# One decoder layer: v kept token by token in DRAM, a bf16 difference in place of a cast, the second close stage's inputs issued by ScalarE, roots ahead of weight remainders

## The reference

```
x = layernorm(x + L0_attn(x))          # qkv = x @ W + b; phi(q), phi(k) = exp(q @ omega - |q|^2 / 2) / sqrt(128)
                                       # y = phi(q) . cumsum(phi(k) v) / (phi(q) . cumsum(phi(k)) + 1e-6); y @ W_proj + b
x = layernorm(x + L0_xattn(x, ctx))    # causal softmax attention, keys and values preceded by 154 rows of ctx; @ W_proj + b
x = layernorm(x + L0_ffn(x))           # 16 routed experts (top 4, in the best 2 of 4 groups) and 2 shared ones
```

## Time and profile before

| | |
|---|---|
| median of 3 runs | 2140.28 us (2139.8 to 2140.62) |
| the profiled execution | 2145.23 us, of which the span from first to last instruction is 2143.2 us |
| granted TensorE clock, mean | 0.940 |
| busy: PE, DVE, ACT, POOL | 87%, 69%, 43%, 21% of the span |
| second close stage with its surroundings (1370 to 1500 us) | 130 us, PE 63% busy |
| first close stage with its surroundings (530 to 690 us) | 160 us, PE 77%, DVE 79% busy |

### The profile page before, as it was taken

The page is one execution under the profiler, slowest core; times in us unless marked ns, Lnnn a source line. Parts: engine busy times, 40 slices in busy tenths (PEclk is TensorE's granted clock), DMA queues, the critical chain, the costliest instruction groups (busy, mean ns, idle before and its releaser), DMA issues. The chain is left out here.

```text
span 2143.2 us, 39212 instructions
## 1 busy us (share of the span) xinstructions
PE 1874.6 (87%) x13696; PEld 1223.8 (57%) x13696; DVE 1484.2 (69%) x3864; ACT 912.8 (43%) x1398; POOL 439.8 (21%) x629
## 2 busy tenths in 40 slices
PE   7948999997885669989989999765799999999997
PEld 4636676775553123333333333243688788888886
DVE  7934455554786758878878888242788877777776
ACT  5524555553332036656656666711323223323322
POOL 2124233211332321112112111254500000000000
PEclk9979999999998579999999999988899999999999
DMA  6989666661687544534534531465400000000000
GB/s 171 220 143 154 108 108 107 111 161 45 174 234 162 87 54 70 80 51 73 79 51 74 78 59 36 121 200 154 135 1 30 30 5 27 30 30 1 20 11 10
DMA packets 161259, 187.38 MB, mean 87 GB/s; under 512 B 74498, under 2 KB 131538, under 8 KB 154942
## 3 DMA queue, kind: packets, MB, share of 16 engines
q1 hardware_dynamic: 135071, 137.56, 28.1%
q0 software_dynamic: 9952, 31.21, 9.7%
q10 hardware_dynamic: 16063, 16.23, 3.4%
HBM read 114.33 MB, written 70.20 MB: 86 GB/s over the span
## 5 line engine op out<-in xcount | busy, mean ns | idle before, releaser
L1406 ACT ACTIVATE sa_prob<-sa_ps_s 128x1024 f32<-128x1024 f32 (+3 forms) x480 | 376.3, 825 | 314.0 <-PE sa_ps_s L1313 193.8
L1466 DVE CUSTOM_DVE_ANT_0 sa_ps_m<-sa_ps_m,sa_later 128x282 f32<-128x282 f32 (+4 forms) x640 | 278.4, 460 | 87.7 <-PE sa_ps_m L1286 86.4
L1469 DVE TENSOR_REDUCE sa_piece_max<-sa_ps_m 128x1 f32<-128x512 f32 x384 | 259.2, 688 | 35.8 <-PE sa_ps_m L1286 35.2
L1286 PE MATMUL sa_ps_m<-sa_k,sa_q 96*128 96x358 bf16 (+7 forms) x1024 | 259.8, 304 | 8.4 <-DVE sa_piece_max L1466 6.7
L1807 DVE SCALAR_TENSOR_TENSOR mo_acc<-mo_ps_o,mo_keep,mo_acc 128x256 f32<-128x256 f32 x512 | 212.2, 476 | 71.8 <-PE mo_ps_o L215 71.6
L1673 ACT ACTIVATE mo_h_hi<-mo_h 128x512 fp32r<-128x512 f32 x144 | 91.0, 632 | 273.0 <-DVE mo_h L1789 270.8
L1444 POOL TENSOR_SCALAR_AFFINE_SELECT sa_prob<-sa_prob 128x256 f32<-128x256 f32 x256 | 102.5, 406 | 509.7 <-ACT sa_prob L1406 507.1
L1313 PE MATMUL sa_ps_s<-sa_q,sa_k 99*128 99x512 bf16 (+3 forms) x768 | 179.7, 330 | 2.1 <-ACT sa_prob L1406 2.0
L1284 PEld LDWEIGHTS sa_ps_m<-sa_km,sa_q 96*128 96x128 bf16 x512 | 50.8, 100 | 218.7 <-issue 124.9
L683 DVE TENSOR_TENSOR la_att<-la_ps_att,la_cap 128x512 f32<-128x512 f32 x128 | 88.3, 690 | 124.8 <-PE la_ps_att L588 124.8
L1286 PEld LDWEIGHTS sa_ps_m<-sa_k,sa_q 96*128 96x128 bf16 x1024 | 99.0, 100 | 127.6 <-DVE sa_piece_max L1466 48.8
(11 more groups left out here) (197 smaller groups left out, 3893.6 us busy)
## 6 DMA issues: line engine op xcount, KB each, us to landing
sa_q<-s_q_parts SPq DMA_DIRECT2D x96, 128.0 KB, 5.0
la_q<-s_q_parts POOLq DMA_DIRECT2D x90, 128.0 KB, 6.1
la_k<-s_k_parts POOLq DMA_DIRECT2D x90, 128.0 KB, 8.2
sa_k<-s_k_parts SPq DMA_DIRECT2D x84, 128.0 KB, 7.5
s_y<-la_y SPq DMA_DIRECT2D x16, 512.0 KB, 3.5
s_x<-cl_xn SPq DMA_DIRECT2D x16, 512.0 KB, 5.8
s_y<-sa_y SPq DMA_DIRECT2D x16, 512.0 KB, 3.2
mw_raw<-experts SPq DMA_DIRECT2D x18, 384.0 KB, 3.9
```

Source lines behind the costliest of these rows:

```text
L1286: last = nc.tensor.matmul(ps_m[:, s, a - lo:hi - lo], qs, k[g][0:STACK, j, a - MEM:hi - MEM], start=lo > 0, stop=True, skip_group_check=True)
L1406: nc.scalar.activation(dst, src, ACT.Exp, scale=HD ** -0.5).then_inc(expd[s], 1)
L1466: nc.vector.tensor_tensor_reduce(ps_m[:, s, 0:hi - lo], ps_m[:, s, 0:hi - lo], later[:, BANK + lo - first:BANK + hi - first], 1.0, -BIG, A ...
L1469: nc.vector.tensor_reduce(piece_max[:, j, t, n:n + 1], ps_m[:, s, 0:hi - lo], AX.X, ALU.max).then_inc(piece_done[s], 1)
```

## The change

Five edits. (1) v is laid out in DRAM token by token, all 16 heads of a token in one row of 272 floats: one DMA per tile stores it with 1088-byte rows, and the attention stages pick 68 of the 272 floats of each row. (2) In stage 1, for the pair (0, 1) only, the second part is computed as a bf16 difference of `full` and the first part, and not as a cast of the float32 remainder; with it one of the two links of the chain of waits is gone, and the order becomes remainder 0, second part 0, remainder 1, second part 1. (3) In stage 2 the inputs of tile n+2 are issued by ACT at the head of its tile n, no longer by SP. (4) In stage 2 POOL takes the root of tile 2b+1 ahead of the weight remainder. (5) The counts that waits on v's stores compare with follow (1).

```diff
@@ project, store of v (close stage 1 has the same)
-                    for t in range(TB):
-                        rows = v_out.rearrange("(i t) w -> i t w", t=T)[bass.ds(b * QUADS, QUADS),
-                                                                        half * TILE + t * P:half * TILE + (t + 1) * P]
-                        sp.dma_start(rows.rearrange("g t w -> t g w"),
-                                     v[:, half, t].rearrange("p (g h) d -> p g (h d)", g=QUADS)).then_inc(v_out_sem[half], 16)
+                    rows = v_out[bass.ds(b * T + half * TILE, TILE)].rearrange("(n p) w -> p n w", p=P)
+                    sp.dma_start(rows, v[:, half].rearrange("p n h d -> p n (h d)")).then_inc(v_out_sem[half], 16)
@@ linear_attention, load_v (softmax_attention has the same)
-            eng.dma_start(v[pr][:, :, :], io["v"][bass.ds(kk * (SLOTS * T) + pr * T, T)]
+            eng.dma_start(v[pr][:, :, :], io["v"][bass.ds(kk * T, T), pr * VW:(pr + 1) * VW]
@@ close_attention, SP
-                    if not on and more:
-                        load_inputs(sp, b, half)
                     sp.wait_ge(normed[half], b + 1 + START)
@@ close_attention, POOL
                 inputs(b + 1, 0)
+                root(*((b + 1, 0) if on else (b, 1)))
                 if not on:
                     weights.remainder(pool, 2 * b)
-                root(*((b + 1, 0) if on else (b, 1)))
                 inputs(b + 1, 1)
@@ close_attention, ACT
-                    if on and more:
+                    if more:
                         load_inputs(act, b, half)
                     act.wait_ge(t_ps, n + 1 + START)
@@ close_attention, DVE, split
                     ins = nc.vector.tensor_tensor(rest[:, s], full[:, s], parts[:, s, 0], ALU.subtract)
+                    if pair[0] == 0:
+                        ins = nc.vector.tensor_tensor(parts[:, s, 1], full[:, s], parts[:, s, 0], ALU.subtract)
                 chain.link(ins)
-                for s in pair:
-                    ins = nc.vector.tensor_copy(parts[:, s, 1], rest[:, s])
-                chain.link(ins)
+                if pair[0]:
+                    for s in pair:
+                        ins = nc.vector.tensor_copy(parts[:, s, 1], rest[:, s])
+                    chain.link(ins)
@@ scratch
-    "v": ((NQ * T, VW), F32),
+    "v": ((B * T, QUADS * VW), F32),
```

More of the change, by code:

```diff
@@ L308, in _ @@
             for half in range(HALVES):
-                sp.wait_ge(v_out_sem[half], 16 * TB * B + START)
+                sp.wait_ge(v_out_sem[half], 16 * B + START)
                 sp.wait_ge(n_out[half], 16 * B + START)
@@ L435, in _ @@
                     dve.wait_ge(v_ps[half], b + 1 + START)
-                    dve.wait_ge(v_out_sem[half], b * (16 * TB) + START)
+                    dve.wait_ge(v_out_sem[half], b * 16 + START)
                     for t in range(TB):
@@ L811, in batch_row @@
                     sp.wait_ge(v_full, tile(b, half) + 1 + START)
[L812 to L817, removed]
+                    rows = io["v"][bass.ds(b * T + half * TILE, TILE)].rearrange("(n p) w -> p n w", p=P)
+                    sp.dma_start(rows, v[:, half].rearrange("p n h d -> p n (h d)")).then_inc(v_out[half], 16)
             for b in range(B):
@@ L824, in _ @@
                 if on:
-                    sp.wait_ge(v_out[half], 16 * TB * B + START)
+                    sp.wait_ge(v_out[half], 16 * B + START)
                 else:
@@ L1051, in copy_v @@
                 dve.wait_ge(v_ps, tile(b, half) + 1 + START)
-                dve.wait_ge(v_out[half], b * (16 * TB) + START)
+                dve.wait_ge(v_out[half], b * 16 + START)
                 for t in range(TB):
@@ L1213, in load_rest @@
             load_stack(eng, km[g], io["mem_parts"], quad_before(b, g), RIGHT, arrived[g])
-            eng.dma_start(v[g][:, :, :], io["v"][bass.ds(b * (QUADS * T) + g * T, T)]
+            eng.dma_start(v[g][:, :, :], io["v"][bass.ds(b * T, T), g * VW:(g + 1) * VW]
                           .rearrange("(n p) w -> p n w", p=P)).then_inc(arrived[g], 16)
@@ L1864 @@
     "q_parts": ((PARTS, B * C, T), BF16), "k_parts": ((PARTS, B * C, T), BF16), "norms": ((PARTS, B * HEADS * 2, T), BF16),
-    "v": ((NQ * T, VW), F32), "y": ((NQ * P, T), F32), "inv": ((B * HEADS, T), F32),
+    "v": ((B * T, QUADS * VW), F32), "y": ((NQ * P, T), F32), "inv": ((B * HEADS, T), F32),
     "score": ((B * T, EXPERTS), F32), "combine": ((B * T, EXPERTS), F32), "x2": ((B * T, C), F32), "x3": ((B * T, C), F32), "xT2": ((B * C, T), F32), "xT3": ((B * C, T), F32),
```

## The result

The changed kernel takes **2188.57 us** (median, 2187.6 to 2193.75) against 2140.45 us (2139.8 to 2141.93) in the same session: ratio 1.0229, 95% interval 1.0211 to 1.0246, so 48 us slower by the medians and 49 by the ratio. Predicted were 2194 us and a range of 2172 to 2206. The profiled execution took 2188.54 us, its span 2186.5 us, against 2143.2 us before.

What follows compares the result with a forecast made beforehand. In the second close stage no engine was taken as the bound, but a chain of waits. Terms 49.0 + 6.1 + 3 - 4 = +54 on a median of 2140.3 gave 2194 us, range 2172 to 2206.

Steps and rivals of the forecast that it cites:

- the ring: Second close stage: load, `yn`, `out_project`, `route`, sigmoid and next load follow one another, 22.7 us per tile; +49.0 us.
- One sign: Second close stage: ACT issues `c_y` within half a microsecond of each sigmoid, six times 22 to 23 us apart.
- (a): First close stage: POOL is not let in between DVE's subtractions, so `normalise` starts 4.2 us earlier; 2164 us, 8%.
- (d): Second close stage: the load is mostly waiting on SP's queue, 7 us on ACT's; +22 us, 2%.
- (c): Second close stage: ACT's load isn't held behind the sigmoid and goes out sooner than from SP; 2134 us, 3%.
- (b): Second close stage: loads are quicker from ACT's own queue, 10.5 us each; 2184 us, 15%.
- Cover of ACT's later copy: Second close stage: ACT's copy of the transposed tile comes 2.4 us later, hidden under the load; 14 us if uncovered.
- Root ahead of the remainder: Second close stage: the root of tiles 1, 3 and 5 comes 1.80 us sooner, worth 0.
- The bf16 difference, +6.1: First close stage: subtractions are held up by POOL like casts, 9.3 us from remainder 0 to `normalise`; +6.1 us.
- the clock, +3: First close stage: more PE idle time makes two more tiles run `out_project` at the 1.2 GHz level; +3 us.
- The sign that I had named: First close stage: second parts take some 1.5 and 3 us, with 9.3 us from remainder 0 to `normalise`.
- v, -4: v's single-DMA stores: -2.5 us at the end of the first close stage, -1.5 at the project stage's; loads 0.

Runs made afterwards that it cites:

- e1: Kernel before, with one edit: ACT instead of SP issues the inputs of the second close stage at the head of its tile; ratio 1.0258.
- after: The changed kernel with all five edits, as profiled, against the kernel before; median 2188.57 us, ratio 1.0229.
- e4: Changed kernel with one edit undone: SP issues the inputs of the second close stage again; ratio 0.9968 to the kernel before.
- e8: Kernel before, with the bf16 difference for pair (0, 1) in the first close stage, but in the old order of operations; single run, 2151.47 us.
- e3: Kernel before, with only v's new DRAM layout and its stores, loads and counts; ratio 0.9976.
- e10: Changed kernel with e9's first close stage, e6's earlier loads, and POOL waiting for `normalise` behind each root in the second close stage; 2101.57 us.
- e11: Kernel before with the bf16 difference in the new order, and POOL's first close stage root computed on 128x256 elements; single run, 2456.57 us.
- e6: Changed kernel with SP issuing the second close stage's inputs a tile earlier (tile n+3 at the head of tile n); ratio 0.9938 to kernel before.
- e9: Kernel before; in the first close stage, POOL's `yn` and `xb` moved beside the copy of v and statistics, ACT's loads a tile earlier; ratio 0.991.

## Why the prediction was right, step by step

- **What bounds close 2, and the ring.** Right. Place and order of all stations came out; the period is 23.2 us (e1) and 23.7 (after), predicted 22.7. The load took 12.7 us on average (12.4), the PE work 8.1 to 8.6 (7.9), and the issue came up to 0.51 us behind the sigmoid (0.04). After 14 us of idle time `out_project`, 6.29 us at 1423.46, has a granted clock of 0.50, the 1.2 GHz level, until past 1428, and 1.00 from 1429 on. The term was +49.0; the stage grew by 50 in e1, by 55 from e4 to after. One sign was put wrongly: not six `c_y` issues but five stand behind a sigmoid, 23.7 to 24.0 us apart and not 22 to 23; tile 2's load does not, as the sum itself had it.
- **Rivals (a) to (d).** (c) and (d) are gone with the timeline of ACT's queue; (b) too: on ACT's queue the loads took 12.2 to 13.2 us, on SP's they had taken 12.0 to 13.5. (a), POOL not let in between subtractions, is excluded by e8 and by second part 1.
- **Cover of ACT's later copy.** It waited 3.0 to 3.6 us for its own queue (2.4 predicted) and is hidden, as said.
- **Root ahead of the remainder.** 0, as said (e3 against e4); that `normalise` would then share its time with the remainder I had not seen.
- **The bf16 difference, +6.1, and the clock, +3.** Wrong; measured -1 (-3 to +1): 8.16 us from remainder 0 to `normalise`, not 9.3, and a slow `out_project` in one of the six tiles (at 592), not in four. The sign that I had named was half there: second part 1 takes 2.85 us, but second part 0 keeps to 0.68 beside the root. The step that failed is the line "root (0.95, what is left of its 1.43)": the root does not hold DVE up. I had also charged for the new second part, and not seen that it falls into the 0.74 us idle time of the earlier trace rows. The rule of the Trainium skill that I cited (SBUF — State Buffer, Who interferes with whom) holds for `yn` and `xb`. The Trainium skill says there as well that a DVE instruction with at most one SBUF input, outside its two-port modes, doesn't contend. The traces agree: in e10 the addition out of PSUM and the statistics took 1.29 and 1.41 us beside POOL. For the root the rule on two SBUF inputs does not hold, as e11 measured.
- **v, -4.** Measured -5 (-7 to -3). From v's last store to the next stage it is 3.4 us less at the end of close 1 (2.5 predicted) and 2.5 less at the end of the project stage (1.5).

The total of 54 against 49 flatters the sum: the ring was taken 6 us too small (49 for 55) and the difference with its clock falls 10 us too large (9 for -1), and these misses cancel in part. That they do is luck; the sign and the size of the change, which the ring alone sets, are not.

## What to carry to other kernels

A DMA issued by a computing engine starts when that engine's program reaches it, not when its own condition holds. Ask what the last wait ahead of it needs; if that needs the load before it, the loads have become serial, and moving the issue up a few lines is worth more than the choice of the engine. Put POOL's large operations beside DVE's work out of PSUM and its statistics, and not beside casts, two-input subtractions or `tensor_scalar`; but first see to it that their loads are there earlier, or the gain turns into a wait for DMA.

## What the runs showed of the hardware

- The operations that POOL's `tensor_tensor` of 128x768 and 128x1024 elements holds up include `tensor_scalar` from SBUF to SBUF (0.35 us each, 8.29 for four beside four POOL operations in e6), and even one of 128x4 elements (0.17 us, 1.73 beside `xb` in e10).
- POOL's power operation took 41.5 us for 128x256 elements (e11) and 1.02 to 1.43 for 128x4, and held DVE up for 0.42 us at most.
- Issuing the four DMAs of 272-byte rows took SP 2.15 us at the end of the stage, 3.5 to 4.7 us in its first five tiles before, and up to 9.26 us in e9; one DMA with 1088-byte rows took 0.37 us in every tile of after and e10. So the same issue does not always cost the same. The DMA share alone does not tell why: it is 0.87 before and 0.90 in e9 from 580 to 620 us, and in e9 the issue at 623 took 2.16 us though the share is 0.85 from 620 to 660. What sets it stays open.
